# A four-layer sequence model on one core: separate tensors for the mean, inverse deviation and shift that ScalarE measures in the first stage

## The reference, cut to what matters

```python
x = x + time_mixing(_layernorm(x))   # RWKV-6, x is (4, 1024, 128); a scan over time with data-dependent decay
x = x + top1_ffn(_layernorm(x))      # 8 experts
x = x + quaternion_memory(_layernorm(x))
x = x + top4_ffn(_layernorm(x))      # 32 experts and a shared one

def _layernorm(x, axis=-1, eps=1e-05):
    m = jnp.mean(x, axis=axis, keepdims=True)
    v = jnp.var(x, axis=axis, keepdims=True)
    return (x - m) / jnp.sqrt(v + eps)
```

## Time and profile before

| what | value |
|---|---|
| median of 3 executions | 820.4 us (819.52 to 821.27) |
| profiled execution, its own time | 819.28 us |
| span of that execution in the trace | 817.3 us |
| busy of the span: PE, DVE, ACT, POOL | 89%, 74%, 59%, 60% |
| mean granted TensorE clock | 0.962 |
| first stage | iteration 0 begins at about 27 us, iteration 1 at about 56 us |

### The profile page before, as it was taken

How to read it: one execution, slowest core, us unless ns; L and a number is a source line. 1 busy time by engine, 2 the same in 40 slices (tenths; PEclk the granted TensorE clock), 3 DMA queues, 4 the chain that set the end, 5 groups by cost and what they waited for, 6 DMA issues and landing times.

```text
span 817.3 us, 14378 instructions
## 1 busy us (share of the span) xinstructions
PE 727.6 (89%) x4027; PEld 549.6 (67%) x4028; DVE 602.2 (74%) x1377; ACT 485.6 (59%) x1045; POOL 490.0 (60%) x498
## 2 busy tenths in 40 slices
PE   4599999999868799668999979999999999999996
PEld 2345554555447689657888867777778787878784
DVE  3489999999965445347888758786868686868673
ACT  3567778664435367446566556666666665666553
POOL 3577668788753544436878745555555555555564
PEclk9889999999979999859999998999999999999999
DMA  8700000000011355210000036363636364646450
GB/s 246 244 0 1 0 1 14 8 8 14 14 40 44 107 137 142 67 41 28 14 1 1 2 74 137 74 149 79 145 83 140 84 140 89 134 93 132 100 122 13
DMA packets 38265, 60.47 MB, mean 74 GB/s; under 512 B 3776, under 2 KB 17728, under 8 KB 37808
## 3 DMA queue, kind: packets, MB, share of 16 engines
q1 hardware_dynamic: 35920, 54.93, 28.5%
q0 software_dynamic: 2272, 4.67, 1.7%
HBM read 51.31 MB, written 8.28 MB: 73 GB/s over the span
## 4 chain that ended last, share of the span: by engine, by line
PE 66%; DVE 17%; issue 7%; ACT 4%; POOL 2%; DMA 2%; DVEq 1%; another core or an unknown queue 0%; ACTq 0%; POOLq 0%; SPq 0%
DVE state_and_wide L803 4%; PE a_vb L635 4%; PE c_m L1861 4%; PE c_m L1826 4%; PE c_m L1863 3%; PE c_m L1862 3%; PE c_r L1842 3%; PE a_front L481 3%; PE a_vb L644 2%; PE a_y L644 2%; DVE a_vb L787 2%; PE c_v L1861 2%; PE c_r L1911 2%; PE c_r L1910 2%; PE c_r L1913 2%
## 5 line engine op out<-in xcount | busy, mean ns | idle before, releaser
L2379 POOL TENSOR_TENSOR d_hid_lo<-c_bound,d_hid_hi 128x512 fp32r<-128x512 f32 x136 | 175.6, 1292 | 141.3 <-ACT d_hid_hi L2289 139.9
L2289 ACT ACTIVATE d_hid_hi<-c_bound 128x512 fp32r<-128x512 f32 x136 | 85.1, 626 | 38.0 <-DVE c_bound L2160 36.8
L1367 POOL TENSOR_TENSOR ducts_and_memory_weights<-a_r,state_and_wide 128x512 f32<-128x512 f32 x64 | 75.0, 1181 | 25.2 <-DVE state_and_wide L803 19.8
L803 DVE TENSOR_TENSOR_SCAN state_and_wide<-a_decay,state_and_wide,a_vb 128x512 f32<-128x512 f32 x64 | 81.0, 1268 | 0.1
L2151 DVE TENSOR_TENSOR c_m<-c_bound,c_m 128x512 f32<-128x512 f32 x64 | 44.3, 691 | 23.5 <-PE c_m L1863 17.5
L2151 DVE TENSOR_TENSOR c_v<-c_bound,c_v 128x512 f32<-128x512 f32 x64 | 44.3, 692 | 22.0 <-PE c_v L1863 16.3
L1861 PE MATMUL c_m<-d_x_hi,d_hi 128*128 128x512 f32 x136 | 56.3, 414 | 3.6 <-DVE c_bound L2160 3.3
L2279 ACT ACTIVATE c_bound<-c_m 128x512 f32<-128x512 f32 x60 | 35.7, 595 | 33.7 <-PE c_m L1863 33.1
L2279 ACT ACTIVATE c_bound<-c_k 128x512 f32<-128x512 f32 x60 | 35.7, 595 | 33.4 <-PE c_k L1863 32.9
L1863 PE MATMUL c_m<-d_x_hi,d_lo 128*128 128x512 f32 x136 | 54.4, 400 | 0.0
L1862 PE MATMUL c_m<-d_x_lo,d_hi 128*128 128x512 f32 x136 | 54.0, 397 | 0.0
(11 more groups left out here) (376 smaller groups left out, 2151.1 us busy)
## 6 DMA issues: line engine op xcount, KB each, us to landing
state_and_wide<-pair_weights SPq DMA_DIRECT2D x64, 512.0 KB, 11.5
b_w<-in_w SPq DMA_DIRECT2D x2, 2048.0 KB, 12.1
state_and_wide<-in_moe SPq DMA_DIRECT2D x16, 204.0 KB
a_xf<-rows_in SPq DMA_DIRECT2D x39, 64.5 KB
state_and_wide<-results SPq DMA_DIRECT2D x8, 256.0 KB, 2.7
out<-c_read SPq DMA_DIRECT2D x8, 256.0 KB, 2.3
a_weights<-in_mixing SPq DMA_DIRECT2D x1, 1077.0 KB, 7.1
shape_consts<-in_consts SPq DMA_DIRECT2D x1, 744.0 KB, 4.4
```

What stands on the lines that cost most here:

```text
L803: dve.tensor_tensor_scan(state[:, j, seq_cols(h, 1)], decay[:, h, :], vb[j % 3][:, :], first, ALU.mult, ALU.add).then_inc(scan_ready, 1)
L1367: pool.tensor_tensor(rs[:, j, :], rr[:, h, :], state[:, j, seq_cols(h, 0)], ALU.mult).then_inc(rs_ready, 1)
L2289: act.activation(hid_hi[:, n % HALVES, :], hidden[:, r, :], ACT.Copy).then_inc(hi_ready, 1)
L2379: pool.tensor_tensor(hid_lo[:, n % HALVES, :], hidden[:, r, :], hid_hi[:, n % HALVES, :].bitcast(F32), ALU.subtract).then_inc(lo_ready, 1)
```

## The change

ACT's mean, and DVE's inverse and shift made from it, get tensors of their own (`minus_measured`, `rstd_measured`, `shift_measured`) and semaphores of their own (`inverse_ready`, `measured`), both counted from the first measured tile. Nothing is computed otherwise, no instruction is moved in any queue, and none but waits are added or taken away. With n = i - 3, ACT's two waits become `need(act, measured, n)` and `need(act, inverse_ready, n)`, which for n = 0 are no waits; DVE's wait for xn is left out for n = 0.

```diff
+        minus_measured = sb("minus_measured", [P, SUB])
+        rstd_measured = sb("rstd_measured", [P, SUB])
+        shift_measured = sb("shift_measured", [P, SUB])
...
+        inverse_ready, measured = sem("inverse_ready"), sem("measured")
...
             def measure(i, h, step):
                 if step == 8:
                     dve.wait_ge(deviation_ready, i - MEASURED + 1)
-                    dve.wait_ge(xn_ready, i)
-                    dve.reciprocal(rstd[:, :], deviation[:, :]).then_inc(rstd_ready, 1)
+                    if i > MEASURED:
+                        dve.wait_ge(xn_ready, i)
+                    dve.reciprocal(rstd_measured[:, :], deviation[:, :]).then_inc(inverse_ready, 1)
                 if step == 9:
-                    dve.wait_ge(rstd_ready, i + 1)
-                    dve.tensor_tensor(shift[:, :], minus_mean[:, :], rstd[:, :], ALU.mult).then_inc(shift_ready, 1)
+                    dve.wait_ge(inverse_ready, i - MEASURED + 1)
+                    dve.tensor_tensor(shift_measured[:, :], minus_measured[:, :], rstd_measured[:, :], ALU.mult).then_inc(measured, 1)
...
                 n = i - MEASURED
                 if step == 1:
                     act.wait_ge(decay_ready, n + 1)
-                    act.wait_ge(shift_ready, i)
+                    need(act, measured, n)
                     for s in range(SUB):
                         a = act.activation(rate[:, s * P:(s + 1) * P], x_tok[:, SUB * i + s, :], ACT.Copy, scale=-1.0 / P,
-                                           accum_out=minus_mean[:, s:s + 1])
+                                           accum_out=minus_measured[:, s:s + 1])
...
-                    act.activation(scaled_mean[:, :], minus_mean[:, :], ACT.Copy, scale=P ** -0.5).then_inc(scaled_ready, 1)
+                    act.activation(scaled_mean[:, :], minus_measured[:, :], ACT.Copy, scale=P ** -0.5).then_inc(scaled_ready, 1)
...
                 if step == 6:
                     act.wait_ge(square_ready, n + 1)
-                    need(act, rstd_ready, i)
+                    need(act, inverse_ready, n)
...
             def norm(i, h, step):
                 if step == (8 if i < MEASURED else 1):
-                    act.wait_ge(shift_ready, i + 1)
+                    if i < MEASURED:
+                        act.wait_ge(shift_ready, i + 1)
+                        by, less = rstd, shift
+                    else:
+                        act.wait_ge(measured, i - MEASURED + 1)
+                        by, less = rstd_measured, shift_measured
                     need(act, xt_ready, i)
                     for s in range(SUB):
                         a = act.activation(xn[:, s, :], x_tok[:, SUB * i + s, :], ACT.Identity,
-                                           bias=shift[:, s:s + 1], scale=rstd[:, s:s + 1])
+                                           bias=less[:, s:s + 1], scale=by[:, s:s + 1])
```

More of the change, by code:

```diff
@@ L339, in seq_cols @@
             return slice(TILE * h + first, TILE * h + first + TILE)
-        taken_over = [sums_ready, scaled_ready, square_ready, deviation_ready, scaled, spread_ready, mean_ready, stats_ready, moments_ready, var_ready, rstd_ready, shift_ready, xn_ready,
+        taken_over = [inverse_ready, measured, sums_ready, scaled_ready, square_ready, deviation_ready, scaled, spread_ready, mean_ready, stats_ready, moments_ready, var_ready, rstd_ready, shift_ready, xn_ready,
                       xt_out, xt_ready, dx_ready, m1_ready, lerp_ready, td_ready, k_ready, rate_ready, decay_ready, v_ready,
```

## The result

Over 19 executions of each, the changed kernel's median is 813.97 us and that of the kernel before 820.42: a ratio of 0.9922 (95% interval 0.9907 to 0.9937), or 6.4 us faster (5.2 to 7.6). The forecast was 7.9 us and 812.5; the measured time lies in the range of 810.5 to 814.6. The profiled execution took 811.47 us, and its span is 809.6 against 817.3. It is the fastest of the 19, so that it meets the 811.4 of the sum is in part luck.

A forecast was written before the change was run, and what follows sets the result against it. The prediction took iteration 0 to be bound by ACT's step-1 wait for POOL's step-4 shift, with four engines idle. v_lo 7.87 us earlier, handed on whole, gave 820.4 - 7.9 = 812.5 us; range 810.5 to 814.6.

The forecast's parts named there:

- The wait, and what comes late next: Iteration 0: without ACT's step-1 wait the Tanh comes 8.1 us earlier; POOL's queue becomes tighter, v_lo 7.87 us earlier.
- The clock term: PE in iteration 0: without the gap its clock stays at 2.4 GHz; second lerp 1.33 us behind the first, not 2.56.
- The edits priced at nothing: ACT's step-6 wait, DVE's step-8 wait, later tiles' semaphores and ACT's remaining wait for POOL's shift: no gain, no cost.
- the cover that I called just enough: ACT behind the Tanh: still waits for POOL's shift, free at about 39.55, just covered before td_hidden's input comes.
- The room at TD2: If ACT's remaining wait were not covered, td_hidden is needed only at matmul TD2: some 2 us of room.
- The rule on the shared interfaces: GpSimd contends with VectorE instructions having two SBUF inputs; the forecast said this case's trace shows no such loss.
- R3: Rival, slower: POOL's run from 36.50 to v_lo takes twice as long beside DVE; 822.3 us, chance 0.02.
- The hand-on to the end: From iteration 1 on nothing is tied to the clock on the wall, so the 7.9 us go to the end.

The follow-up runs named there:

- e3: Changed kernel with ACT's step-1 wait for POOL's shift put back for tile 3 alone; iteration 0 28.99 us, ratio 1.0009 to the kernel before.
- e2: Kernel before with only ACT's mean in its own tensor and ACT's step-1 wait of tile 3 dropped; iteration 0 21.14 us, ratio 0.9907.
- e9: Changed kernel with DVE's statistics of tile 2 left out; iteration 0 took 20.36 us, against 21.13.
- e10: Changed kernel without DVE's statistics of tile 2 and without POOL's four instructions on that tile; iteration 0 took 19.71 us, against 21.13.
- e4: Changed kernel, but ACT's step 1 for tile 3 waits for DVE's moments of tile 2; iteration 0 26.32 us, ratio 0.9960.
- e7: Kernel before with six spare PE matmuls in its wait for z of tile 6, iteration 7; ratio 1.0024, iteration 0 28.45 us.
- e1: The changed kernel itself run again; 806.22 us against 811.25 for the kernel before, ratio 0.9914.
- e11: The changed kernel itself run once more, beside a kernel with spare PE matmuls; ratio 0.9891 to the kernel before.
- e5: Changed kernel with twelve groups of four spare DVE statistics instructions spread over iterations 1 to 6; 3.4 us faster than the kernel before.

## Why the prediction was right

*The wait, and what comes late next.* Right step by step: ACT from xt straight to measuring, no wait on PE at the first lerp, v_lo 9.79 us behind the third product (9.81 forecast), iteration 0 shorter by 7.89 (7.87 forecast). e3 and e2 pin it to ACT's step-1 wait, e9 and e10 to POOL's queue as the next bound.

*The clock term.* Right: the second lerp came 1.24 us behind the first (1.33 forecast), and e4 shows that 1.3 us are lost when PE does go idle. The trace that the forecast was read from paid the full 1.3 us, and that is chance: by e7's trace the gain is 7.3 us and not 7.9 (28.45 - 21.13).

*The edits priced at nothing.* Right: e2 leaves two of the tensors out and loses nothing, although the cover that I called just enough (ACT free at 39.55 for td_hidden) was used up there: ACT came to td_hidden without a wait, 0.4 us later than in the changed kernel. The room at TD2, PE's matmul from td_hidden, held.

*The rule on the shared interfaces.* Half wrong. POOL's instructions kept their length (2.14 and 2.15 us for two), and R3 did not come. But I wrote that this case's trace shows no such loss, having read POOL's rows alone. DVE pays: its shift took 0.60 us in place of 0.15, and the trace of the kernel before already had such a case, both below. It was free here only because POOL was the tighter queue. (Both engines idled together for 4.9 us before, 37.59 to 42.48, not for over 5.) By the Trainium skill (GPSIMD Engine Reference, 1. Specifications) a VectorE instruction with two SBUF inputs contends; the trace agrees, with 0.45 us for this one.

*The hand-on to the end.* Right within the measurement, with a remainder. The four ratios of kernels with the full effect and nothing added (changed, e1, e2, e11), weighted by their intervals and taken as independent, give 0.9914 +- 0.0011, which is 7.0 us of 820 (6.1 to 7.9): the forecast 7.9 stands at the edge, and the main comparison alone (5.2 to 7.6) leaves it just outside. e5's dose (2.9 us by its stretches, 3.4 measured) and e4's (2.7 against 3.2) show no loss on the way. Three things could make up the 0.9 us, and none is shown. Executions like e7's, whose stall cost 0.6 us less, would lower the mean gain, and how many there are is unknown. Among the experts, whose stretch scatters by several us for the same code, the changed kernels took longer than the stalled one in both sets that have a trace of each without fillers (115.04 against 111.13; 106.90 and 105.25 against 104.41). And the clock around the hand-over, which I held to be the cause for a while, is not shown to be one.

## What to carry to other kernels

A small tensor that two producers share in turn can tie a whole pipeline stage together: look for the wait that guards its reuse, and at which step of the other engine's program it is met, here step 4 from step 1. When such a stall goes, add up the queue of every engine that stood still with it, since the slowest queue, not the stall, gives the gain; here that sum came out right to 0.02 us. A stall that lets PE go idle also has a price in clock, and this price is not the same in every execution (0.75 to 1.3 us here): one trace is not enough for it. Compare stretches between named instructions of the traces, which repeated to 0.1 us in the stage that was changed, but for that price, before looking for 1% in totals that scatter by as much.

## What the runs showed of the hardware

A DVE instruction with two SBUF inputs was held until POOL's running instruction ended. It is the shift of tile 3, 128x4, whose two operands both lie in SBUF. DVE and POOL in e9_no_stats:

```profile
41.66 0.87 DVE L769 TENSOR_TENSOR a_shift_measured<-a_minus_measured,a_rstd_measured 128x4 f32<-128x4 f32 x1
```

```profile
41.42 2.13 POOL L1367 TENSOR_TENSOR a_xf<-a_lerp,a_xt 128x512 f32<-128x512 f32 x2
```

POOL's two instructions of 1.09 us each start at 41.42 and about 42.47; the shift starts at 41.66 and ends at 42.53, just behind the end of the first (42.51). In the changed kernel it runs from 43.05 to 43.65 and POOL's first xf of that pair ends at about 43.62. In e10_no_pool_stats POOL idles at that moment, and the shift takes its usual time:

```profile
42.68 0.16 DVE L769 TENSOR_TENSOR a_shift_measured<-a_minus_measured,a_rstd_measured 128x4 f32<-128x4 f32 x1
```

It was 0.15 us in the kernel before and in e3, where POOL idled too (until 50.85 in the earlier trace rows), and 0.60 to 0.62 in all kernels that had the full effect and DVE's statistics. The lerps and scans beside it, with one operand in PSUM, kept their lengths. So did three short ones of the routing in the changed kernel (L941, L948, L953, one operand in PSUM each): 0.19, 0.16 and 0.18 us at 115.74, 117.87 and 120.32, each inside a running product, xf or v_lo of POOL.

The kernel before has a case too. `climb` (L901) is a difference of two parts of one small SBUF tensor:

```profile
229.02 0.69 DVE L901 TENSOR_TENSOR a_climb<-a_first_rows 128x7 f32<-128x7 f32 x1
```

```profile
228.61 1.08 POOL L1367 TENSOR_TENSOR ducts_and_memory_weights<-a_r,state_and_wide 128x512 f32<-128x512 f32 x1 [0.45 <-DVE state_and_wide L803]
```

It ends at 229.71, POOL's product at 229.69; a subtraction of about that size, 128x8 with both operands in SBUF (L879, at 225.80), took 0.17 us with no arithmetic of POOL beside it.
